# A transformer on one core: the router turned round, a bias folded into a projection, POOL's copies moved forward

## The reference, cut to what matters

```python
out_lat = merge(o_lat) @ Wo_lat + bo_lat           # 32 tokens
out_ctx = merge(o_ctx) @ Wo_ctx + bo_ctx           # 998 tokens
h = h + concatenate([out_ctx, out_lat], axis=1)
x = layernorm(h)                                   # mean and variance over 192
logits = x @ w_router.T                            # 8 experts
scores = softmax(logits); selection = scores + expert_bias
top_idx = top_k(selection, 2)                      # the two experts of a token and their shares
h = h + routed experts(x) + (silu(x @ sg.T) * (x @ su.T)) @ sd.T      # the last is the shared network
```

## Time and profile before

| | us |
|---|---|
| median of 3 runs (4458.52 to 4472.81) | 4466.18 |
| the profiled execution, its own time | 4471.9 |
| its span in the trace | 4470.2 |
| mean granted TensorE clock over the span | 0.929 of full speed |
| PE, DVE, ACT, POOL busy over the span | 3951.7, 2508.2, 1440.9, 1271.0 |

### The profile page before, as it was taken

How to read it: one execution, slowest core, us unless ns; L and a number is a source line. 1 busy time by engine, 2 the same in 40 slices (tenths; PEclk the granted TensorE clock), 3 DMA queues, 4 the chain that set the end, 5 groups by cost and what they waited for, 6 DMA issues and landing times. The chain is left out here.

```text
span 4470.2 us, 74427 instructions
## 1 busy us (share of the span) xinstructions
PE 3951.7 (88%) x23896; PEld 2418.5 (54%) x23898; DVE 2508.2 (56%) x4595; ACT 1440.9 (32%) x2892; POOL 1271.0 (28%) x1439
## 2 busy tenths in 40 slices
PE   8899878699999998564999999999995998899996
PEld 8788555466666666332233333333333675577774
DVE  1576467632222222685887787778862547644442
ACT  0222110011111111233477777777772221111110
POOL 0221010134444443455000001000012112177775
PEclk9999998899999999776799999999996889999998
DMA  6221111223333331246232233322215431277776
GB/s 223 59 65 54 31 39 29 80 62 62 62 65 65 66 66 24 85 138 148 43 55 45 45 46 58 52 45 45 45 28 128 126 89 42 75 175 173 173 173 153
DMA packets 335969, 361.69 MB, mean 81 GB/s; under 512 B 50412, under 2 KB 297155, under 8 KB 334143
## 3 DMA queue, kind: packets, MB, share of 16 engines
q1 hardware_dynamic: 252207, 274.75, 25.2%
q0 software_dynamic: 61312, 63.66, 9.2%
q10 hardware_dynamic: 22288, 20.93, 1.5%
HBM read 247.51 MB, written 117.00 MB: 82 GB/s over the span
## 5 line engine op out<-in xcount | busy, mean ns | idle before, releaser
L2033 DVE TENSOR_REDUCE at_mx<-psum 128x1 f32<-128x998 f32 (+1 forms) x768 | 884.8, 1190 | 253.4 <-PE psum L1858 253.0
L1988 ACT ACTIVATE at_p<-psum 128x512 f32<-128x512 f32 (+3 forms) x1536 | 851.4, 588 | 299.2 <-PE psum L1932 269.1
L1932 PE MATMUL psum<-at_q,at_k 99*128 99x512 bf16 (+3 forms) x1536 | 521.5, 382 | 21.4 <-issue 16.4
L1858 PE MATMUL psum<-at_k,at_q 96*128 96x512 bf16 (+3 forms) x1536 | 475.6, 392 | 70.5 <-POOL at_identb L1815 33.1
L1918 PE MATMUL psum<-at_p,at_v 128*32 128x486 f32 (+3 forms) x3072 | 406.9, 602 | 1.0 <-ACT at_p L1988 0.7
L1932 PEld LDWEIGHTS psum<-at_q,at_k 99*128 99x128 bf16 (+1 forms) x1536 | 155.6, 102 | 426.2 <-ACT at_p L1988 272.0
L1224 DVE TENSOR_TENSOR ex_hT<-ex_silu,psum 128x384 f32<-128x384 f32 (+1 forms) x288 | 147.6, 512 | 415.8 <-ACT ex_silu L1193 270.6
L1193 ACT ACTIVATE ex_silu<-psum 128x384 f32<-128x384 f32 (+1 forms) x288 | 131.5, 456 | 772.9 <-PE psum L1137 642.8
L1830 POOL DMA_DIRECT2D o_rows<-at_o x96 | 48.5, 505 | 1145.5 <-DVE at_mx L2033 872.7
L1159 PE MATMUL psum<-ex_wd,ex_hT 128*128 128x192 f32 (+1 forms) x1728 | 291.5, 327 | 0.0
L1858 PEld LDWEIGHTS psum<-at_k,at_q 96*128 96x128 bf16 (+1 forms) x1536 | 152.4, 105 | 232.7 <-DVE at_mx L2033 64.0
(11 more groups left out here) (378 smaller groups left out, 7067.5 us busy)
## 6 DMA issues: line engine op xcount, KB each, us to landing
mx_wd<-in_e_dT SPq DMA_DIRECT2D x72, 288.0 KB, 4.1
qk_parts<-hd_parts SPq DMA_DIRECT2D x32, 579.4 KB, 3.8
at_k<-qk_parts SPq DMA_DIRECT2D x144, 128.8 KB, 5.4
at_q<-qk_parts SPq DMA_DIRECT2D x144, 124.8 KB, 4.6
tok_p<-in_x SPq DMA_DIRECT2D x12, 1176.0 KB
mx_wg<-in_e_gT SPq DMA_DIRECT2D x72, 192.0 KB, 2.5
mx_wu<-in_e_uT SPq DMA_DIRECT2D x72, 192.0 KB, 2.8
v_rows<-hd_v_out SPq DMA_DIRECT2D x8, 1536.0 KB
```

The source lines that it names most:

```text
L1858: mm = pe.matmul(psum[0:ctx_rows[t], 3 + 2 * ((PRO + n) % 2) + k, 0:w], Q[v][0:R6, j * 1024 + 128 * t:j * 1024 + 128 * t + ctx_rows[t]], K ...
L1932: pe.matmul(psum[0:n, i % RING, 0:w], K[u][:, j, 128 * t:128 * t + n], Q[u][:, j * 1024 + at:j * 1024 + at + w], start=True, stop=True).th ...
L1988: act.activation(P[0:n, c % 2, j, 0:w], psum[0:n, i % RING, 0:w], ACT.Exp).then_inc(exp_ready, 1)
L2033: dve.tensor_reduce(mx[0:ctx_rows[t], j * CT + t:j * CT + t + 1], pair(n)[0:ctx_rows[t], 0:CTX], AX_X, ALU.max).then_inc(s_free, 1)
```

## The change

Four things are altered. (1) The router is the stationary operand and the tokens stream past it: one matmul of up to 512 columns for each cut and feature half, six an image; the logits come out as [8 x 1030] of an image, ACT copies them to `lT` cut by cut between the evictions, and a DMA (`store_logits`) puts them into their eight rows of `logits`, which is now [64 x 1030]. `phase_dispatch` turns them back with nine transposes on PE and three copies on DVE. Cut s is routed once transposes and evictions 0 to 3 + s are done, and after ACT has taken the cut before. (2) The bias is worked out in row 64 of `wo_g`, the weights of the second feature half, and row 64 of `op` holds ones; `add_bias` is gone, with what waited for it. (3) POOL's `pair_up` stands first in each turn and at the head of `phase_dispatch`. (4) ACT evaluates a silu of one column (`warm`) right behind the square root; its loop is a Python loop; and `root` of the next image now stands behind the logits and their store. SP's loads no longer wait for the memsets.

```diff
         queue.dma_start(c["bias"][:, n, :], spread(inp[f"L1_attn_bo_{name}"], 128)).then_inc(arrived, 16)
-    for dst, src in ((c["router"][:, 0, :], inp["routerT"][0:128]), (c["router"][0:64, 1, :], inp["routerT"][128:D]),
...
     NJ, NX = len(JOBS), DC * len(CUTS)
     LOAD = 16 * (3 + 2 + HEADS)
...
 
...
-            pool.memset(hin[:, :, 7:NT, :], 0.0).then_inc(zeroed, 1)
+            pool.memset(eps[:], EPS).then_inc(zeroed, 1)
             pool.memset(mv[:], 0.0).then_inc(zeroed, 1)
-            pool.memset(eps[:], EPS).then_inc(zeroed, 1)
             pool.memset(xn[:, 7:NT, :], 0.0).then_inc(zeroed, 1)
...
-            pool.wait_ge(bias_ready, 1)
-
-            def add_bias(i, half):
-                pool.wait_ge(loaded[half], i * LOAD + LOAD)
-                pool.tensor_tensor(hin[:, half, 0:8, :], hin[:, half, 0:8, :],
-                                   bias[:, 0:1, :].to_broadcast([128, 8, D]), ALU.add).then_inc(bias_added, 1)
-                pool.wait_ge(bias_added, 2 * i + half + 1)
-                pool.tensor_tensor(hin[0:LAT, half, 8, :], hin[0:LAT, half, 8, :], bias[0:LAT, 1, :], ALU.add) \
-                    .then_inc(hb_ready[half], 1)
-                pool.wait_ge(hb_ready[half], i + 1)
 
...
+                pool.tensor_copy(x3T[1][rows, b // 2, :], xT[64:128, 1, :]).then_inc(xT_kept, 1)
...
-            for n in range(2):
-                add_bias(0, n)
             keep(0)
-            add_bias(1, 0)
             pair_up(0)
             keep(1)
             for i in range(1, FUSED):
-                add_bias(i, 1)
+                pair_up(i)
                 keep(2 * i)
-                add_bias(i + 1, 0)
-                pair_up(i)
                 keep(2 * i + 1)
-            add_bias(FUSED, 1)
             keep(B - 2)
             keep(B - 1)
...
+            pe.wait_ge(bias_ready, 1)
...
-            def route(b):
-
-                pe.wait_ge(xT_ready, b * NX + NX)
-                pe.wait_ge(l_ready, b)
-                for t, at, n in TC:
-                    for k, r in enumerate(WIDTH):
-                        mm = pe.matmul(psum[0:n, 7, t * E1:(t + 1) * E1],
-                                       xT[0:r, k, at:at + n], router[0:r, k, :], start=(k == 0), stop=(k == 1))
+            def route(b, s):
+                at, w = CUTS[s]
+
+                pe.wait_ge(xT_ready, b * NX + len(CUTS) + s + 1)
+                pe.wait_ge(l_ready, b * len(CUTS) + s)
+                for k in range(2):
+                    mm = pe.matmul(psum[0:E1, 7, 0:w], router[:, k, :], xT[:, k, at:at + w], start=(k == 0), stop=(k == 1))
                 mm.then_inc(l_full, 1)
+
+            def turn_and_route(b, first):
+                for k in range(first, NX):
+                    turn(b, k)
+                    if k > len(CUTS):
+                        route(b, k - len(CUTS) - 1)
+                route(b, len(CUTS) - 1)
...
-            for k in range(NX):
-                turn(0, k)
-            route(0)
+            turn_and_route(0, 0)
             pe.wait_ge(dispatch_in, DISPATCH_CONSTS)
-            pe.wait_ge(bias_ready, 1)
...
@@ -2410,9 +2398,7 @@
                 for k in range(3):
                     up(i, 3 + k)
                     turn(n - 1, k)
-                for k in range(3, NX):
-                    turn(n - 1, k)
-                route(n - 1)
+                turn_and_route(n - 1, 3)
...
-                for k in range(NX):
-                    turn(n, k)
-                route(n)
-            for k in range(NX):
-                turn(B - 1, k)
-            route(B - 1)
+                turn_and_route(n, 0)
+            turn_and_route(B - 1, 0)
...
                 m, (at, w) = k // len(CUTS), CUTS[k % len(CUTS)]
                 if k == 0:
                     act.wait_ge(xT_kept, b)
-                    act.wait_ge(l_full, b)
+                    act.wait_ge(l_full, b * len(CUTS))
                 act.wait_ge(xT_full, b * NX + (k + 1))
-                act.activation(xT[0:WIDTH[m], m, at:at + w], psum[128 - WIDTH[m]:128, 2 + k % 2, 0:w], ACT.Identity) \
-                    .then_inc(xT_ready, 1)
-
-            def take_logits(b):
-                act.wait_ge(l_full, b + 1)
-                for t0, t1, n in ((0, 7, 128), (7, 8, CTX - 896), (8, 9, LAT)):
-                    last = act.activation(tiles_logits[0:n, t0:t1, bass.ds(b, 1), :].rearrange("p t a e -> p t (a e)"),
-                                          psum[0:n, 7, t0 * E1:t1 * E1].rearrange("p (t e) -> p t e", e=E1), ACT.Identity)
-                last.then_inc(l_ready, 1)
+                act.activation(xT[:, m, at:at + w], psum[:, 2 + k % 2, 0:w], ACT.Identity).then_inc(xT_ready, 1)
+
+            def take_logits(b, s):
+                at, w = CUTS[s]
+                if s == 0:
+                    act.wait_ge(l_stored, b * 16)
+                act.wait_ge(l_full, b * len(CUTS) + (s + 1))
+                act.activation(lT[:, at:at + w], psum[0:E1, 7, 0:w], ACT.Identity).then_inc(l_ready, 1)
+
+            def take_turned_and_logits(b, first):
+                for k in range(first, NX):
+                    take_turned(b, k)
+                    if k > len(CUTS):
+                        take_logits(b, k - len(CUTS) - 1)
+                take_logits(b, len(CUTS) - 1)
+
+            def store_logits(b):
+                act.wait_ge(l_ready, b * len(CUTS) + len(CUTS))
+                act.dma_start(logits[b * E1:(b + 1) * E1], lT[:]).then_inc(l_stored, 16)
 
             def root(b):
                 act.wait_ge(moments_ready, b + 1)
                 act.activation(std[:], mv[:, :, 1], ACT.Sqrt, bias=eps[:]).then_inc(std_ready, 1)
+
+                act.activation(warm[:], eps[:], ACT.Silu)
...
@@ -2475,34 +2468,31 @@
             root(0)
             store_x3(0)
             store_h3(1)
-            for k in range(NX):
-                take_turned(0, k)
-            take_logits(0)
+            take_turned_and_logits(0, 0)
+            store_logits(0)
             root(1)
             store_x3(1)
-            with act.Fori(0, FUSED) as i:
+            for i in range(FUSED):
                 n = i * 2 + 2
                 silus(i, range(3))
                 store_h3(n)
                 for k in range(3):
                     silus(i, (3 + k,))
                     take_turned(n - 1, k)
-                for k in range(3, NX):
-                    take_turned(n - 1, k)
+                take_turned_and_logits(n - 1, 3)
+                store_logits(n - 1)
                 root(n)
-                take_logits(n - 1)
                 store_x3(n)
 
                 silus(i, range(6, UP))
                 store_h3(n + 1)
-                for k in range(NX):
-                    take_turned(n, k)
+                take_turned_and_logits(n, 0)
+                store_logits(n)
                 root(n + 1)
-                take_logits(n)
                 store_x3(n + 1)
-            for k in range(NX):
-                take_turned(B - 1, k)
-            take_logits(B - 1)
+            take_turned_and_logits(B - 1, 0)
+            store_logits(B - 1)
+            act.wait_ge(l_stored, 16 * B)
             act.wait_ge(h3_stored, 48 * B)
             act.wait_ge(x3_stored, 48 * B)
...
-                    dve.wait_ge(hb_ready[half], i + 1)
...
-            dve.memset(op[64:128, :, 1, :], 0.0)
-            dve.memset(wo_g[64:128, :, 1, :], 0.0)
+            dve.memset(op[64:128, :, 1, :], 0.0).then_inc(ones_ready, 1)
+            dve.memset(wo_g[64:128, :, 1, :], 0.0).then_inc(ones_ready, 1)
+            dve.memset(router[0:64, 1, :], 0.0)
             dve.wait_ge(consts_in, PROJECT_CONSTS)
             dve.tensor_copy(shifts[:], shift[:].to_broadcast([128, 128])).then_inc(shifts_ready, 1)
             for f, (_, r) in enumerate(FEATS):
                 last = dve.tensor_scalar(wo_g[0:r, :, f, :], wo[0:r, :, f, :], gain[0:r, 0:1], None, ALU.mult)
             last.then_inc(wo_ready, 1)
+            dve.wait_ge(ones_ready, 2)
+            dve.memset(op[64:65, :, 1, :], 1.0).then_inc(ones_ready, 1)
             dve.wait_ge(shift_full, 1)
-            dve.tensor_tensor(bias[:], psum[:, 5:7, 0:D], bias[:], ALU.add).then_inc(bias_ready, 1)
+            dve.tensor_tensor(wo_g[64:65, :, 1, :], psum[64:65, 5:7, 0:D], bias[64:65], ALU.add).then_inc(bias_ready, 1)
...
+            def pair_up(g):
+
+                pool.wait_ge(u_full, g * UP)
+                pair_of(pool, x3T[1], xr, g + FUSED, xr_ready, g)
+
+            pair_up(0)
+            pool.memset(tiles[:, 7 * B:, :], 0.0).then_inc(zeroed, 1)
             pool.memset(zero[:], 0.0).then_inc(zeroed, 1)
             pool.memset(zerob[:], 0.0).then_inc(zeroed, 1)
             pool.memset(ones[:], 1.0).then_inc(zeroed, 1)
 
             pool.memset(slot[:], -1e6).then_inc(zeroed, 1)
-            pool.wait_ge(zeroed, 4)
+            pool.wait_ge(zeroed, 5)
...
-
-            def pair_up(g):
-
-                pool.wait_ge(u_full, g * UP)
```

(19 more changed lines are left out.)

20 lines of the change are left out of this document (10 added, 10 removed).

## The result

The kernel after takes 4480.97 us (median of 20 runs, 4467.89 to 4490.32), the kernel before, timed beside it, 4473.02 (20 runs, 4458.52 to 4481.55). The ratio is 1.0020, 95% interval 1.0011 to 1.0029: slower by 8 us by the medians and 9 by the ratio, small but clear of the scatter, and within the 0.3% that the prediction called the same. The forecast was 4469 in a range of 4454 to 4482. It was built on 4466.18, the median of three runs of before; the median of twenty is 4473.02, so 7 of the 12 us between forecast and measurement lie in that base and not in the change. The profiled execution of after took 4482.68 us, its span is 4480.7.

What follows compares the result with a forecast made beforehand. In the middle and at the end of each turn the chain behind routing was taken to hold PE, elsewhere PE bounds. Terms of -5.8 us plus +8.4 for the clock gave +2.6 on median 4466.2: 4469, range 4454 to 4482.

Steps and rivals of the forecast that it cites:

- rival (b): PE's clock falls at each of six gaps and stays low, 3.75 us each: 4483 us; chance 0.09.
- Rival (a): PE itself is the bound, not the chain behind routing: about 4425 us, partial form 4451; chance 0.13 for both.
- The new routing and its chain: Each routing takes 5.5 us at full clock, then root to `mult` 8.2 us, with `norm` at 2.68.
- Three middles: Middle routing of a turn, from old routing start to `up(i, 7)`: +0.8 us each, +2.4 together.
- The ends: Routing at a turn's end with a network behind it, twice: -1.8 us each, -3.6 together.
- The clock: PE stands idle behind five routings and then runs slower: +1.68 us each, +8.4 together.
- Rival (c): PE's clock never falls in the gaps: -5.8 us, 4460.4; chance 0.13.
- rival (d): Silu's table load held ACT longer than its record; five chains gain up to 1.4 us more each: 4462; chance 0.05.
- POOL's moved pair: POOL's two copies now run while DVE multiplies: between 0 and 2.1 us three times, taken as 0.
- The head of `phase_dispatch`: DVE's chain to the first `mult` ready at 10.9 us of the phase, less 0.2 overlap, against 12.0: -1.3 us.
- The start: Start of `phase_project`: -4.5 us down to routing 0, then -2.9 from there to `up(0, 1)`.
- The last two images: From routing 6 to the next phase: +4.1 us; +2.2 at full clock, +5.5 if it stays low.

Runs made afterwards that it cites:

- e1: The kernel after with the next image's square root issued ahead of the logits' copies and silu's table load split off behind it; 0.9954 of before.
- e5: The kernel after with ACT issuing the first silu behind each routing of the loop ahead of `store_x3`; root still behind the logits; 0.9975 of before.
- e2: The kernel after with four or five extra 512-column matmuls, results unused, in PE's idle stretch behind each routing of the loop; 0.9978 of before.
- e9: The kernel after with POOL's bias addition, POOL's old order and SP's wait for the first loads back; 1.0022 of before.
- e3: The kernel before with only the bias row, POOL's copies for the network first and the first loads without a wait; 0.9980 of before.
- e10: e1 with the bias, POOL's order and the first loads as in the kernel before; 1.0030 of before.
- e8: The kernel after with silu's table load back behind `store_x3`, in silu's way; 1.0030 of before.
- e4: The kernel before with only the next image's square root moved behind the logits' copies, in the loop and at the turn's end; 1.0058 of before.

## Why the prediction was right, and where its steps were off

**What bounds the kernel: right.** The chain behind each routing holds PE, as forecast: five idle gaps of 4.8 to 5.3 us (forecast 5.3 and 4.7), released by `mult`, none at a table load. The clock's mean over the stretch of the earlier trace rows rose from 0.84 to 0.90, so the sign that was set for rival (b), a mean below 0.84, did not come. e1 and e5 shorten the chain without touching PE's work and gain 29 and 20 us. Rival (a), PE as the bound, is out: PE has 18 us less to do and the phase is longer.

**The new routing and its chain: right to the tenth.** Routing 5.35 us against 5.5, the chain behind it 8.21 against 8.2, `norm` 2.68 everywhere, clock 1.00 through the routing. Busy time of the routing 4.3 us against 4.5, with two waits for ACT in it. Three middles: +1.7 against +2.4.

**The ends: mis-sized.** `store_x3` was put at its 1.66 us of the middle; at the ends it took 2.31 and 2.42. The DMA share in those issues was 0.97 and 1.04, in the middle 0.40. That is 1.4 of the 2.2 us by which -3.6 came out as -1.4; the rest was not traced.

**The clock: the term that was mis-sized.** "The nearest row: after a gap of 4.46 us the same 18 matmuls took 4.05 instead of 2.37, +1.68", "Five such gaps: +8.4", and the reason, "whose gap is nearly as long". Measured were 2.6 to 2.9 in after, +13.9. One row was taken for a constant, and it was too short to show the whole price: at half clock 2.37 us of work can lose 2.4 us and no more, while 3.4 to 5.2 us of work stood behind each of the five gaps. The same row in after:

```profile
3886.05 4.50 PE L2806 MATMUL psum<-di_hot_hi,di_hot_lo 128*128 128x288 bf16 x18 [4.46 <-DVE di_hot_hi L3012]
```

The gap is the same to 0.01 us, and the loss is 2.13 instead of 1.68. Here the clock is 0.50 to the last matmul; in before it was back at 1.00 within the row (0.50 up to 3880 us, 0.80 in the microsecond behind). This gap is 4.46 us in all fourteen profiled kernels, and the matmuls behind it took from 3.99 to 4.50. Ahead of the units measured here, gaps of 2.9 us and more cost between 1.5 and 3.1, as the last section shows. In hindsight the middle between 1.68 and the 3.75 of the other bound, 2.7, would have served; no row of before gave it. That e2 gains 13.2 us by filling the gaps shows that this term is the clock's. Rival (b), 3.75 a gap, was too high; the measured mean, 2.8, lies midway between forecast and rival, and below the 3.2 from which the prediction let (b) decide. Rival (c), a clock that never falls, is out.

**What was removed from the chain: right in size, wrong in its reason.** The prediction took `norm`'s 3.5 us of contention as something that the bias row frees. e9 shows that in the middle the late root alone already leaves POOL's addition behind; e3, that in the old order it was hidden by PE at the low clock. Behind `up(0, 1)` the bias row pays only in the early-root order, and there it is worth 21 us. The start, where SP's wait goes with it, was 8 us shorter in e1 than in e10 and in e3 than in before, but 2 in after than in e9. The table load is worth its own 1.28 us, as e8 shows; rival (d) is out. That the Trainium skill, "ScalarE: Activation LUTs", section "What ACT_TABLE_LOAD costs", puts a switch at about 2.66 us with a drain, does not fit these rows.

**POOL's moved pair: right, nothing.** `mult` took 0.37 us under the pair's copies at 3507.07 and 0.37 alone at 3499.11. `norm`, which reads one tensor, and that from SBUF, did suffer under POOL: 4.35 us under its copies (e1), 7.94 under its copies and its addition (e10). By the rule that the prediction took from the Trainium skill, "SBUF — State Buffer", section "Who interferes with whom", an instruction with one SBUF input contends only in a two-port mode, and the section names `tensor_scalar`, which `norm` is, among those that can enter one. The rows of `mult` fit the rule; those of `norm` fit it if `norm` ran in such a mode, which no run here shows.

**The head of `phase_dispatch`: right at its first `mult`, the end not settled.** Its `mult` came at 10.51 us of the phase against 12.03, -1.5 where -1.3 was forecast; then the clock fell again (0.73 from 3705 to 3710 us) and the phase ended 2.1 us late. Yet e4, whose `phase_dispatch` is that of before, took 205.5 us for it where before took 202.6, and the kernels with the new one took from 200.4 (e1) to 204.8 (e2). The 2.1 is inside what the same code scatters, and so is the forecast's -1.3: these runs decide neither.

**The start** was given -7.4 and measured -6.1; e4, with the old start, came 2.2 us sooner to `up(0, 1)` than before did, so this too is inside the scatter. **The last two images** were given +4.1 and took +2.6: the last routing came 3.1 us later behind the one ahead of it than before, where some 4 were forecast, and took 6.2 us, not 7.4.

The total was forecast at +2.6, and is +8 by the medians. In the two phases it came out as +12.0, 9 more than forecast, of which the clock is 5.5, `phase_dispatch` 3.4 and the ends 2.2. That the total lies nearer to the forecast is in part luck: the last two images, the remainder and the phases that were not touched took 1.5, 0.8 and 1.5 us less. The range held, at its edge, because rival (b) had been let into it; without the 7 us by which the base of three runs was low it would have held with room.

## What to carry to other kernels

When a wide engine's work shrinks, follow the chain that it used to cover: here eight routings gave PE 18 us of freedom, and a square root placed behind three copies took it all back. Order on the engine that issues the chain (root early, silu ahead of stores, stores where the queues are calm) and a second bank took the kernel from 1.0020 to 0.9879 of before without one instruction less on PE. And a gain from taking away contention has to be priced in the order that the kernel will have: behind `up(0, 1)` the bias row was worth nothing in the old order (e3), nothing with the root late (e9) and 21 us with the root early (e10).
